# Layer 1's keys, values, later queries and scores as streams of their own, in a new order of steps

## The reference

```python
x = ln(x + L0_attn(x))           # 16 heads of 8, causal
x = ln(x + L0_xattn(x, ctx))     # 8 heads of 16, over the context
x = ln(x + L0_ffn(x))            # 64 experts, top 6, and a shared expert
x = ln(x + L1_attn(x))           # 16 heads of 64, causal, biases on q, k and v
x = ln(x + L1_xattn(x, ctx))     # 16 heads of 64, over the context
x = ln(x + L1_ffn(x))            # in truth an attention: 8 heads of 16 over nested widths
```

## Time and profile before

| | |
|---|---|
| timed runs | 2020.08 us median of 3 (2018.52 to 2020.89) |
| span of the profiled execution | 2015.1 us |
| TensorE busy | 1709.3 us, 85% |
| VectorE, ScalarE, GpSimd busy | 56%, 44%, 11% |
| TensorE's granted clock, mean | 0.929 |
| first matmul of phase 3 | 695.17 us |

### The profile page before, as it was taken

The page is one execution under the profiler, slowest core; times in us unless marked ns, Lnnn a source line. Parts: engine busy times, 40 slices in busy tenths (PEclk is TensorE's granted clock), DMA queues, the critical chain, the costliest instruction groups (busy, mean ns, idle before and its releaser), DMA issues.

```text
span 2015.1 us, 45063 instructions
## 1 busy us (share of the span) xinstructions
PE 1709.3 (85%) x19224; PEld 1111.5 (55%) x19224; DVE 1122.6 (56%) x2308; ACT 894.8 (44%) x1641; POOL 230.1 (11%) x392
## 2 busy tenths in 40 slices
PE   3778787778669599899899889989979989989985
PEld 2444444444468456556556656655745655665663
DVE  5566677766764453663663564465365366366343
ACT  2444445445422244454454454544455445435442
POOL 0000110001136200200100010010010010011000
PEclk9987889878979799899999999989989989999997
DMA  7300000000076500000000010010000000000000
GB/s 276 145 22 26 20 15 22 26 26 5 13 159 87 159 20 4 19 25 3 20 25 2 3 43 3 3 40 5 2 22 22 4 20 25 3 2 7 1 2 6
DMA packets 51303, 66.95 MB, mean 33 GB/s; under 512 B 6599, under 2 KB 41905, under 8 KB 50243
## 3 DMA queue, kind: packets, MB, share of 16 engines
q1 hardware_dynamic: 47971, 60.23, 9.2%
q0 software_dynamic: 2560, 3.46, 1.9%
q10 hardware_dynamic: 576, 0.39, 0.1%
HBM read 41.73 MB, written 24.12 MB: 33 GB/s over the span
## 4 chain that ended last, share of the span: by engine, by line
PE 71%; DVE 13%; ACT 10%; issue 3%; DMA 2%; POOL 1%; SPq 0%; ACTq 0%; DVEq 0%; POOLq 0%; PEldq 0%
PE psum L568 8%; PE psum L940 6%; PE psum L833 6%; PE psum L731 5%; DVE peak L1218 4%; ACT prob L1095 4%; PE psum L581 3%; PE psum L820 3%; PE psum L791 3%; PE psum L593 3%; PE psum L893 3%; PE psum L726 2%; PE psum L630 2%; PE psum L637 2%; DMA xz<-x_res 2%
## 5 line engine op out<-in xcount | busy, mean ns | idle before, releaser
L1095 ACT ACTIVATE prob<-psum 128x1024 f32<-128x1024 f32 (+2 forms) x384 | 339.9, 915 | 280.1 <-PE psum L720 96.8
L1218 DVE TENSOR_REDUCE peak<-psum 128x4 bf16<-128x1024 f32 (+2 forms) x176 | 210.1, 1219 | 57.5 <-PE psum L677 28.1
L1218 DVE TENSOR_REDUCE w_shared<-psum 128x4 bf16<-128x1024 f32 x128 | 155.5, 1227 | 142.3 <-PE psum L637 142.3
L1388 POOL TENSOR_TENSOR rstd<-moments,eps 128x2 f32<-128x2 f32 x80 | 15.6, 195 | 1347.7 <-DVE moments L1136 1347.7
L940 PE MATMUL psum<-w_late,qt 128*128 128x128 f32 x1024 | 140.7, 299 | 0.1
L940 PEld LDWEIGHTS psum<-w_late,qt 128*128 128x128 f32 x1024 | 132.4, 211 | 13.4 <-issue 10.9
L568 PE MATMUL psum<-xt,w_late 128*128 128x256 f32 x512 | 133.1, 404 | 5.6 <-ACT xt L1014 4.7
L731 PE MATMUL psum<-qt,kt 64*128 64x256 f32 x1024 | 131.4, 376 | 0.0
L833 PE MATMUL psum<-prob,v_big 128*64 128x256 f32 x1024 | 124.6, 385 | 0.0
L1201 DVE TENSOR_REDUCE w_shared<-psum 128x8 bf16<-128x512 f32 x64 | 41.3, 688 | 144.2 <-PE psum L644 144.2
L568 PEld LDWEIGHTS psum<-xt,w_late 128*128 128x128 f32 x512 | 93.1, 196 | 37.9 <-issue 12.7
(11 more groups left out here) (262 smaller groups left out, 3098.9 us busy)
## 6 DMA issues: line engine op xcount, KB each, us to landing
zd<-kx SPq DMA_DIRECT2D x24, 512.0 KB, 5.6
union<-zd SPq DMA_DIRECT2D x16, 768.0 KB, 4.8
xg<-union SPq DMA_DIRECT2D x16, 192.0 KB, 2.0
w_late<-in_w1T SPq DMA_DIRECT2D x1, 2816.0 KB, 12.7
kt<-in_w2T SPq DMA_DIRECT2D x4, 704.0 KB
union<-in_x SPq DMA_DIRECT2D x16, 128.0 KB, 2.2
union<-in_xT SPq DMA_DIRECT2D x16, 128.0 KB, 2.5
xtd<-x_out SPq DMA_DIRECT2D x16, 128.0 KB, 2.0
```

Source lines behind the costliest of these rows:

```text
L1095: nc.scalar.activation(prob[s][:, slot + 2 * i:slot + 2 * i + 2, 0:n], v.pair(step, i)[:, :, 0:n], ACT.Exp, scale=a.scale).then_inc(v.free ...
L1218: nc.vector.tensor_reduce(dst, src, axis=AX.X, op=ALU.max).then_inc(v.free(step), 1)
```

## The change

Six streams instead of four. C and D get, behind F's three steps, the `early_steps` of L1: XT, K 0 to 3, Q 2 and 3, C1, S 4 to 7. E and F are the four V steps of each sequence. The main chains A and B begin with Q 0 and 1, C0, S 0 to 3, N. The order of turns is new, as are the counts of ahead steps: (16, 25, 15, 15, 4, 4) for (27, 13, 4, 4). The list still has 170 steps. The new order puts one sequence's early and value steps beside the other's and its own L1X and L1F, T and P of L1/b ahead of the body's end, and Z and Y at its begin.

```diff
     if a is L1:
-        first = st("Q", 0, 1) + st("K", 0, 1) + st("C", 0)
-        second = st("Q", 2, 3) + st("K", 2, 3) + st("C", 1)
-        out = first + woven(st("S", 0, 1, 2, 3), second) + woven(st("S", 4, 5, 6, 7), st("V", 0, 1, 2, 3))
+        out = st("Q", 0, 1) + st("C", 0) + st("S", 0, 1, 2, 3)
...
+def early_steps(s):
+
+    st = lambda kind, *n: [(kind, L1, s, i) for i in n]
+    return [("XT", L1, s, 0)] + st("K", 0, 1, 2, 3) + st("Q", 2, 3) + st("C", 1) + st("S", 4, 5, 6, 7)
...
-    front = lambda s: [("Z", "F", s, 0), ("Y", "F", s, 0), ("L", "F", s, 0), ("XT", L1, s, 0)]
+    front = lambda s: [("Z", "F", s, 0), ("Y", "F", s, 0), ("L", "F", s, 0)] + early_steps(s)
+    values = lambda s: [("V", L1, s, i) for i in range(4)]
...
-    return [main(s) for s in AB] + [front(s) for s in AB]
+    return [main(s) for s in AB] + [front(s) for s in AB] + [values(s) for s in AB]
...
-TURNS3 = ("B A B2 A2 B A B A2 B A5 B2 A2 B A2 B A2 B4 A B A5 B2 A2 B3 A B2 A B2 A2 B4 A2 B A3 B2 A2 B2 A B7 A "
-          "B A B A C B2 A B2 A B2 A B A2 B A C A B2 A B A2 C B C A B A B A B A3 B A2 B2 D A B A3 B2 D A D A B "
-          "A2 B A B D A B4 A B A2 B A B A B2 A B A B2 A B A B2 A4")
-AHEAD1, AHEAD3 = (33, 26, 0, 0), (27, 13, 4, 4)
+TURNS3 = ("A2 B4 A D A B D2 A2 B A B A2 B5 A D A B A2 B C D2 B2 A B2 C B A2 D A C F B A3 C B A D C A C B A B A "
+          "B A2 B A2 B D B F E A2 D C B2 F B2 E D A B A B A B F C D2 A C D A2 E B2 A3 B A B A C E D B A C B2 A "
+          "B2 A2 B C A B A B2 A2 B A3 C B C A B4 C B A B2 A B A B2 A B3 A B A2 B A2 B A3 B A")
+AHEAD1, AHEAD3 = (33, 26, 0, 0), (16, 25, 15, 15, 4, 4)
...
-        km = {L0: [t[:, 0:4, :] for t in kt], L1F: [t[:, 0:2, :] for t in kt],
+        km = {L0: [t[:, 0:4, :] for t in kt], L1F: [kx_ab[:, s, :].rearrange("p (i k) -> p i k", i=2) for s in AB],
               L0X: [t[:, 4, 0:128].rearrange("p (i k) -> p i k", i=2) for t in kt]}
         kx0 = [t[:, 7, 0:CTX] for t in kt]
-        x_ffn = [t[:, 7, :].rearrange("p (t d) -> p t d", t=2) for t in kt]
-        att = [t[:, 5, :].rearrange("p (t d) -> p t d", t=2) for t in kt]
...
+        att_f = [t[:, 0:4, :].rearrange("p a k -> p (a k)").rearrange("p (t d) -> p t d", t=2) for t in vx]
+        att_f_t = [t[:, 4:8, :].rearrange("p a k -> p (a k)") for t in vx]
+        att = {L0: att0, L0X: att0, L1F: att_f}
...
                 elif a is L1:
+                    if i == 0:
+                        pe.wait_ge(*v.drained(("XT", a, s, 0)))
...
                 if a is L1 and which == 4:
-                    pe.wait_ge(y.q16[s], v.q_cast(a, 1))
-                    pe.wait_ge(y.k16[s], v.k_cast(a, 1))
+                    pe.wait_ge(y.q16_early[s], v.once())
+                    pe.wait_ge(y.k16_early[s], v.once())
...
                 pe.wait_ge(*v.drained(("S", a, s, len(S_STEPS[a]) - 1)))
+                if a is L1:
+                    pe.wait_ge(*v.drained(("S", a, s, 3)))
...
-                    if i == 3:
-                        act.wait_ge(y.res_ready[s], v.attn(L1))
...
             elif kind == "Y" and more:
-                sp.wait_ge(y.f_link[s], v.at(3, 2))
+                sp.wait_ge(y.f_link[s], v.at(3, 1))
+                load_routed(sp, seq + 2, s)
+            elif kind == "Q" and a is L1 and step[3] == 0 and more:
+                sp.wait_ge(*v.drained(("XT", L1, s, 0)))
+                sp.wait_ge(y.res_ready[s], v.attn(L1))
                 load3(sp, seq + 2, s)
-                load_routed(sp, seq + 2, s)
```

More of the change, by code:

```diff
@@ L340, in decoder_program @@
         rec = pair("rec", [128, 32])
-        km = {L0: [t[:, 0:4, :] for t in kt], L1F: [t[:, 0:2, :] for t in kt],
+        km = {L0: [t[:, 0:4, :] for t in kt], L1F: [kx_ab[:, s, :].rearrange("p (i k) -> p i k", i=2) for s in AB],
               L0X: [t[:, 4, 0:128].rearrange("p (i k) -> p i k", i=2) for t in kt]}
         kx0 = [t[:, 7, 0:CTX] for t in kt]
-        x_ffn = [t[:, 7, :].rearrange("p (t d) -> p t d", t=2) for t in kt]
-        att = [t[:, 5, :].rearrange("p (t d) -> p t d", t=2) for t in kt]
-        att_t = [t[:, 6, :] for t in kt]
+        x_sum = [t[:, 7, :].rearrange("p (t d) -> p t d", t=2) for t in kt]
+        x_ffn = x3_in
+        att0 = [t[:, 5, :].rearrange("p (t d) -> p t d", t=2) for t in kt]
+        att0_t = [t[:, 6, :] for t in kt]
+        att_f = [t[:, 0:4, :].rearrange("p a k -> p (a k)").rearrange("p (t d) -> p t d", t=2) for t in vx]
+        att_f_t = [t[:, 4:8, :].rearrange("p a k -> p (a k)") for t in vx]
+        att = {L0: att0, L0X: att0, L1F: att_f}
+        att_t = {L0: att0_t, L0X: att0_t, L1F: att_f_t}
         heads_out = [t[:, 2:4, :].rearrange("p a b -> p (a b)") for t in qt]
@@ L433, in decoder_program @@
         ATTN_PER = {"p1": 2, "p3": 3}
-        CASTS_Q = {L0: 1, L0X: 2, L1: 1, L1X: 3, L1F: 5}
-        CASTS_K = {L0: 1, L0X: 2, L1: 1, L1X: 3, L1F: 4}
-        CASTS_PER = {("p1", "q"): 2, ("p3", "q"): 5, ("p1", "k"): 2, ("p3", "k"): 4}
+        CASTS_Q = {L0: 1, L0X: 2, L1: 1, L1X: 2, L1F: 4}
+        CASTS_K = {L0: 1, L0X: 2, L1: 1, L1X: 2, L1F: 3}
+        CASTS_PER = {("p1", "q"): 2, ("p3", "q"): 4, ("p1", "k"): 2, ("p3", "k"): 3}
         NARROW = {L0: 1, L0X: 2, L1F: 1}
@@ L911, in tensor_step @@
                 for t in range(2):
-                    last = nc.tensor.transpose(bank[:, 128 * t:128 * t + 128], att[s][:, t, :], ident[:, :])
+                    last = nc.tensor.transpose(bank[:, 128 * t:128 * t + 128], att[a][s][:, t, :], ident[:, :])
                 last.then_inc(v.full(step), 1)
@@ L933, in tensor_step @@
                         p = 64 * (e % 2)
-                        last = mm(bank[p:p + 64, (e // 2) * 128:(e // 2) * 128 + 128], att_t[s][:, 64 * e:64 * e + 64],
+                        last = mm(bank[p:p + 64, (e // 2) * 128:(e // 2) * 128 + 128], att_t[a][s][:, 64 * e:64 * e + 64],
                                   wf_o[:, e, :], start=(e < 2), stop=True, skip_group_check=True)
@@ L946, in tensor_step @@
                     for t in range(2):
-                        last = mm(bank[:, t * 128:(t + 1) * 128], att_t[s][:, t * 128:(t + 1) * 128], w,
+                        last = mm(bank[:, t * 128:(t + 1) * 128], att_t[a][s][:, t * 128:(t + 1) * 128], w,
                                   start=True, stop=True)
@@ L1052, in scalar_step @@
                     act.wait_ge(*v.drained(("Q", a, s, 0)))
-                copy(flat(qb[s][:, c, :]), flat(qt[s][:, c, :])).then_inc(y.q16[s], 1)
+                cast = y.q16_early[s] if a is L1 and half == 1 else y.q16[s]
+                copy(flat(qb[s][:, c, :]), flat(qt[s][:, c, :])).then_inc(cast, 1)
                 if a is L0 or a is L1F:
@@ L1115, in scalar_step @@
                 act.wait_ge(*v.filled(step))
-                copy(att_t[s], v.bank(step)[:, 0:256]).then_inc(v.free(step), 1)
+                copy(att_t[a][s], v.bank(step)[:, 0:256]).then_inc(v.free(step), 1)
             elif kind == "R1":
@@ L1160, in vector_step @@
                     dve.wait_ge(*v.drained(("K", a, s, 2 * step[3] + 1)))
-                    nc.vector.tensor_copy(flat(kb[s][:, c, :]), flat(kt[s][:, c, :])).then_inc(y.k16[s], 1)
+                    cast = y.k16_early[s] if step[3] == 1 else y.k16[s]
+                    nc.vector.tensor_copy(flat(kb[s][:, c, :]), flat(kt[s][:, c, :])).then_inc(cast, 1)
                 elif a is L0 or a is L1F:
@@ L1348, in vector_step @@
                 if not v.first():
-                    dve.wait_ge(y.x_ready[s], v.ln(L1X) - LN_PER["p3"])
+                    dve.wait_ge(y.x_ready[s], v.ln(L1) - LN_PER["p3"])
                 dve.wait_ge(y.routed_in[s], v.at(16, 16))
-                nc.vector.tensor_reduce(x_ffn[s], routed[s].rearrange("p t k d -> p t d k"), axis=AX.X,
+                nc.vector.tensor_reduce(x_sum[s], routed[s].rearrange("p t k d -> p t d k"), axis=AX.X,
                                         op=ALU.add).then_inc(y.f_link[s], 1)
@@ L1356, in vector_step @@
                 dve.wait_ge(y.x_in[s], v.at(16, 16))
-                tt(x_ffn[s], x_ffn[s], x3_in[s][:, :, :], ALU.add).then_inc(y.f_link[s], 1)
+                tt(x_ffn[s][:, :, :], x_sum[s], x3_in[s][:, :, :], ALU.add).then_inc(y.f_link[s], 1)
                 dve.wait_ge(y.f_link[s], v.at(3, 2))
```

11 lines of the change are left out of this document (7 added, 4 removed).

## The result

The kernel after takes 1934.06 us in the median (1931.34 to 1937.28, four runs), beside 2019.3 us (2011.79 to 2020.89, four runs) for the kernel before: a ratio of 0.9584, with an interval from 0.9569 to 0.9599. The forecast was 1960 us in a range from 1932 to 2003, so the direction is right, the time lies in the range, but only 2 us above its lower end, and 26 us of the gain were not foreseen.

The account below looks back on a forecast made before the run. TensorE bound the kernel, with VectorE taking over narrowly in one stretch. Terms: 695.2 + 2.0 + 81.5 + 7 x 152.5 + 109 = 1955.2 us of span, and 5.0: 1960 us, range 1932 to 2003.

Parts of the forecast that it names:

- the prediction's own signs: Bodies 150-155 us, TensorE idle 6-9 us, clock at least 0.99, rdiag under 1.2, run-up 79-86, last body 103-116.
- Idle time: TensorE's waits in a body: 6.4 us from placing steps plus 1.1 for hand-overs, 7.5 against 12.6 before.
- VectorE as the bound: From D of L1X/a to N of L1/b VectorE takes over by little, 46.4 us against 45.9 of matmul.
- Half clock: Time lost in a body to the 1.2 GHz level: 0.7 us remaining of 5.3, bounds 0 and 5.3.
- The rival of a clock that still falls once a body: Half clock keeps costing 5.3 us: body 157.1 us, 1992 us in all; chance 0.20.
- Work: TensorE's warm matmul in a body, 143.7 us plus 0.6 for seams, 144.3, taken as unchanged by the new order.
- Ramps: Last phase's run-up 81.5 us for 38.38, last body 109 for 145.90, and 2.0 more for a later load before them.
- Around the span: Constant of 5.0 us by which the median of timed runs exceeds the span, carried unchanged.
- The shared port: VectorE applies meeting POOL's residual adds cost 0.4 us each, perhaps 2.4 a body, 17 in all; only in the range.
- Better cover: Rival: waits behind VectorE merge, 3.5 us idle and no half clock, body 147.8, 1927 us; chance 0.13.
- Banks that VectorE empties: Rival: V steps' PSUM banks are emptied late, 12 us more a body plus half clock, 169.1, 2076 us; chance 0.08.
- No gain: Rival: waits move without shrinking, body 162.2 us, only the ramps are left, 2028 us; chance 0.07.

Follow-up runs that it names:

- experiment 3: Kernel after with the eight V steps of a body put back beside T of their own sequence; 2013.19 us, 0.9725 of the kernel before.
- experiment 6: Three attempts on the w_shared wait; the third, kernel after with VectorE's L1 and L1F maxima over half the columns: 1929.26 us, 0.9554 of the kernel before.
- experiment 2: Kernel before with sixteen unread matmuls in the rdiag wait: 2039.55 us, 0.9857; with sixteen more in the x_norm wait: 2050.09 us, 0.9883.
- experiment 7: Kernel after with D of L1/a taking its reciprocal three times instead of once; 2013.95 us, 0.9726 of the kernel before.
- experiment 4: Kernel after with early K and Q steps of L1 moved back behind L1F's S steps; 2044.67 us, 0.9867 of the kernel before.
- experiment 5: Kernel after with D of L1/a queued ahead of Y and L of the FFN; 1975.81 us, 0.9547 of the kernel before.

## Why the prediction was right, and where it was off

The direction and the cause were right: cover for TensorE's waits, and with it the clock. The time lies in the range with 2 us to spare, since idle time, clock, work and the constant around the span all erred the same way. Two of the prediction's own signs didn't come: the body is 149.0 us, where 150 to 155 was to show it right, and `rdiag` is on top of the waits with 1.42 us, where it was to be under 1.2. Idle time, clock, run-up and last body came out as the signs said.

**Idle time (7.5 a body forecast, 6.4 measured).** Placing the steps one by one found the two longest waits in their places: B0 of L1/a, 1.0 forecast and 1.42 measured; the group of A2, W, N0 of L1/b and T0.0 of L1/b, 2.05 forecast, 0.46 for `vx` and 1.05 for `w_shared` measured. N to T0 of L1F/b (0.5) is the 0.48 for `shift_n`. ScalarE's run of exponentials (0.9) cost 0.20 + 0.23, the stretch between T1 of L1F/b and V3 of L1/a (0.8) 0.27 + 0.39, the latter at A1 of L1F/b for ScalarE's `qt`, W0, T0 and T1 in L1F's second half (0.55) 0.24 + 0.19. The `x_norm` of L1F/b (0.4) isn't waited for any more; P1 of L1X/a beside it waits 0.41 for ScalarE. One was not in the list: 0.41 of K0 of L1/b for a bank of ring M that `summed` empties.

**VectorE as the bound: wrong.** The forecast had VectorE at 46.4 us against 45.9 of matmul from D of L1X/a to N of L1/b. The window of that stretch has 45.86 us of TensorE, as forecast, but 39.06 of VectorE in 48.63. The operations were counted nearly right: their lengths in the window add up to 43.0 us, where I had 44.1. The waits for POOL were right too, 3.3 us where I had 3.6, as VectorE's waits in that window show:

```profile
DVE x_norm L1160 <- POOL rstd L1408: 1.8, 1, 1.8
DVE x_out L1166 <- POOL rstd L1408: 1.5, 1, 1.5
```

The step that failed is the 3% taken off for the overlap of neighbours in VectorE's queue: 43.0 us of operations cover only 39.06, which is 9%. With the waits for POOL that is 42.4 us, under TensorE's 45.86 and not above it. The two longest waits were found nevertheless, for each was worked out from a local queue, not from the total. That its total isn't the bound is shown twice: fewer values in its dense stretch made the body longer (experiment 3), and 12 us less work for it shortened the body by 1 (experiment 6).

**Half clock (0.7 forecast, 0 measured).** The clock stayed up although the longest wait is 1.42 us, where none was to be over 1.1. Experiment 2 shows in the kernel before that the half clock follows idle time, experiment 7 in the kernel after that it would come back behind a wait of 3.4 us. The rival of a clock that still falls once a body is refuted. How wide the margin is, no run shows: experiment 4 holds 1.00 in six of seven bodies with a wait of 1.9 and 11.9 us idle, and the kernels of experiment 2 have drops behind 1.64 and 1.02.

**Work (144.3 forecast, 142.6 measured): the largest miss.** The step that was mis-sized is this term: I took the work of the kernel before, with its seams, as one that the new order can't change. It can: at a clock of 1.00 the busy time is 144.1 in experiment 2 (145.97 less the filling's 1.91), 144.4 in experiment 3 and 144.6 in experiment 4, with 11.2, 8.7 and 11.9 us idle, and 142.6 with 6.4 in the kernel after. It doesn't go with the idle time, for experiment 5 has 5.3 idle at the same 142.55. It goes with how often TensorE waits: waits of over 0.1 us number 21, 19 and 20 a body in experiments 2, 3 and 4, and 13 in the kernel after and in experiment 5. That the edges of the matmul groups at each wait are the reason is argued, not shown, for these runs also differ in which steps are neighbours. This term alone is 1.7 x 7 = 12 us; with 1.1 of idle and 0.7 of clock it is 3.5 a body, 24.6 us of the 26.

**Ramps.** Run-up 83.5 for 81.5, last body 108.7 for 109, first matmul of the phase 696.0 for 697.2: within 2 us each. **Around the span** 1932.91 - 1931.1 = 1.8 us and not the 5.0 that I carried from a median and another execution's span: 3.2 us.

**The shared port** didn't show as a loss. Of ten pairs of applies in a body four took 0.93 to 1.01 us in the kernel before, each beside an add on POOL, and two do now: 0.99 beside the add at 1247.83, above, and 0.93. A third, beside an add at 1324.40, takes 0.60 us but starts after a wait of 1.52, where the same pair in the kernel before waited 1.16:

```profile
1324.89 0.60 DVE L1166 TENSOR_SCALAR x_out<-summed,moments,rstd 128x128 f32<-128x128 f32 x2 [1.52 <-POOL rstd L1408]
...
1336.68 0.93 DVE L1166 TENSOR_SCALAR x_out<-summed,moments,rstd 128x128 f32<-128x128 f32 x2
```

So there are three meetings for four, by no design that I can show. The Trainium skill (SBUF — State Buffer, Who interferes with whom) says that whichever of the two issues first has the shared ports for its whole instruction and that the other is blocked meanwhile. The rows agree that the two disturb each other; they don't show that the rest of the add is what is lost, as the prediction had it. At 1299.54 that rest is 0.66 us and the pair lost 0.40; at 1247.90 it is 0.65 and the pair lost 0.39.

**The rivals.** Better cover, at 147.8 us a body, was nearest to the 149.0 measured, though not by its mechanism: idle time is 6.4, not 3.5, and the work term made up the difference. Banks that VectorE empties are refuted: `v_big` is in no wait, and of the banks of ring M that VectorE empties only one is waited for, 0.4 us for `summed`. No gain is refuted by every body.

**Better than both.** The kernel after with D of L1/a ahead of Y and L of the FFN (experiment 5) runs at 0.9547 and 0.9543 of the kernel before, where the kernel after has 0.9603 in the session of the first: 1975.81 against 1986.56 us, of which 1.14 x 7 = 8.0 us are seen in the bodies.

## What to carry to other kernels

Count idle time of the bound engine, the clock that it loses by it, and the busy time that comes with waits as three prices of the same thing: here the new order took 6.2 of 12.6 us of idle time, all of the 5.3 of half clock, and 1.7 of busy time a body. Find a wait by the queue of its producer at that place, not by the producer's total: VectorE, at 58% busy, was late twice a body, yet taking 12 us of work off it gave 1 us. Before moving a step to end a wait, look who is second: D ahead of Y won 1.14 of 1.42 us, since only 0.28 us stood behind it, and three attempts on `w_shared` won little, since ScalarE was ready only 0.3 us earlier than VectorE.

## What the runs showed of the hardware that I had not expected

Useless matmuls made a kernel faster: sixteen of them, 1.91 us, in a wait of 2.1 us, and five of seven bodies were 5.1 us shorter, by the clock. The Trainium skill (TensorE: Matmul & The Clock Gate, A second HAM failure mode: psum-queue depth-cycling) tells of a kernel in which short idle time between groups of matmuls comes often enough for the clock to swing; the bodies of the kernel after, with 6.4 us idle in waits of up to 1.42 us, hold 1.00, and the filled kernel with both waits covered did fall to 0.50, so the rows bear the rule out in one kernel and not in the other.

The clock doesn't repeat itself: behind the same two waits of 1.64 and 1.02 us it fell in some bodies of an execution and not in others, in the kernel before and in both filled ones. And one program took some 57 us longer in another session before phase 3 starts, while its bodies agree to 0.1 us. In the two traces of the kernel after, the first product of `v_big` and `w_shared` in phase 2 starts at 573.23 and 572.95 us and the first matmul of phase 3 at 696.04 and 753.07, so the difference arises between these two; its cause is open.
